# Flamingo block on one core: the order within a slot changed on VectorE, ScalarE and GpSimd, and another interleaving at the end

## The chip, the cores and the metric

The kernel runs on one core of a Trainium2 chip. The metric is the device time of one execution in microseconds (us). TensorE (PE) multiplies matrices, VectorE (DVE) and ScalarE (ACT) do elementwise work and reductions, GpSimd (POOL) a few small operations and some transfers, SyncE (SP) only issues transfers (DMAs).

## The reference

32 sequences x of 128 tokens by 128 channels, each with a context of 77 rows by 96. Cross-attention with 16 heads of 8 channels on the twice normalised x, added back through tanh of a gain; then a mixture of 8 experts of which each token uses 2, added back likewise:

```python
x = x + jnp.tanh(g_xattn[0]) * xattn(_layernorm(x), ctx_768, norm_g, norm_b, tnorm_g, tnorm_b, Wq, bq, Wk, bk, Wv, bv)
#   q = (layer_norm(x) @ Wq + bq), k, v = layer_norm(xf) @ Wk + bk, @ Wv + bv; H = 16, hd = 8
#   w = softmax(q k / sqrt(hd)); y = w v
x = x + jnp.tanh(g_ffn[0]) * ffn(_layernorm(x), w_router, w1, w2)
#   logits = xf @ w_router; top_vals, top_idx = top_k(logits, 2); probs = softmax(top_vals)
#   h = square(relu(xf w1[e])); y_e = h w2[e]; out = sum over the chosen two of y_e * probs
```

## The kernel before

The 32 sequences are cut into S = 8 groups of G = 4 (called s); one sequence of a group is a batch, j = 0 to 3. The program is a software pipeline written out by hand, with one instruction stream for each engine. `steps` runs a step for i = -2 to S + 1, and a step has four slots j. In slot j of step i, `slots` (line 253) names the batches in work: near[k] is the batch k slots away from batch j of group i. For near[2] the maxima of the scores are taken, near[0] gets its transposed scores (scoresT) and exponents, near[-1] the products with v (values), the turn of its heads and the post work on VectorE, near[-2] its transpose (turn), its logits (route) and the low part of x. Beside this, two experts of an older group are computed per slot (`ffn_units`, line 247): hidden (TensorE), gated (u, VectorE), square (hs, ScalarE), output (TensorE); e[1] and e[2] are the two experts, and held is the last expert of the slot before, whose output comes at the start of this slot. From i = 8 on only closing work is left. For the last group the experts are weighed afterwards by `weighed` and have no gates before.

TensorE's tiles for scores, transposes and projections share two banks in turn (`ab_sequence`, line 45): each use waits until the use two before it has been taken (`claim`), unless it is marked free because another wait implies that. Names that follow: negm (line 1003) is the maximum over one part of the scores, s1a to s1d are four parts of a batch, of which a and b come at the end of one slot, c and d at the start of the next. `attended` (line 1017) is the post work in steps: rden, o, x1 (written x<-x_res,o), st, mv. `rstd` on GpSimd makes rs from mv, `normalise2` makes xn from both, `turn` (line 559) transposes xn, `routed` (line 1060) takes top and logits. `gate` (line 1069) makes the gates of a group in slot 1. TensorE turns them (line 574), ScalarE copies them, SP stores them in DRAM and broadcasts them back as gb in three parts, and `gated` (line 1116) reads gb in slot 2. `low_keys` and `low_queries` make k_lo and q_lo in slot 3. `load_rows` (line 1300) is GpSimd's transfer x_res, read by x1 a step later; `load` fetches x and context for three groups ahead in slot 1, behind rstd.

VectorE's stages are Python generators: `take(stage, n)` issues the next n pieces of a stage, so the order of VectorE is the order of the take lines in its `step` (line 1194). Nothing is scheduled automatically.

## Time and profile before

| | |
|---|---|
| time, median of 3 runs (lowest, highest) | 349.1 us (348.03, 349.65) |
| the profiled execution | 348.87 us, of which the span shown is 347.1 |
| TensorE busy | 292.9 us, 84% of the span |
| VectorE, ScalarE, GpSimd busy | 66%, 52%, 31% |
| mean granted TensorE clock | 0.966 of full speed, full speed in each whole step after the start |

A busy time says little about which engine to blame here, since all engines work at once. Read how much TensorE idles in one step, then which instruction of another engine ended each idle time, and then what stood ahead of that instruction on its own engine. In a timeline row the bracket is the idle time ahead of the instruction and what ended it; durations of neighbours can overlap a little, since an engine starts the next instruction while the last one drains.

### The profile page before, as it was taken

The numbers are of one execution on the slowest core, as the hardware profiler recorded it, in microseconds if no ns is written. First come the engines' busy times: TensorE is split into PE (matmuls) and PEld (weight loads), VectorE is DVE, ScalarE is ACT, GpSimd is POOL, SyncE is SP. The second block draws the span as 40 slices with busy tenths as digits, with TensorE's granted clock in tenths as the row PEclk, the third lists the DMA queues.
The fourth block names the chain that finished last, engine by engine and source line by source line (L and its number), as shares of the span: only waits on it lengthen the run. The fifth ranks groups of instructions, "written<-read, shape, count | busy, mean of one in ns | idle before, by whom it ended". The sixth has DMA issues, their size and how long they took to land.

```text
span 347.1 us, 7792 instructions
## 1 busy us (share of the span) xinstructions
PE 292.9 (84%) x2809; PEld 237.6 (68%) x2809; DVE 230.6 (66%) x929; ACT 181.0 (52%) x412; POOL 109.2 (31%) x198
## 2 busy tenths in 40 slices
PE   0867979888889998999899989999999999787695
PEld 0435658666767877777777777777777788675484
DVE  7565275677757775778677757886657656554555
ACT  1331354656455566555655566466556555553373
POOL 6495305147303531343134313421322100211000
PEclk9995587999999999999999999999999999999999
DMA  3243011027343836283629281835273530350011
GB/s 82 79 128 111 19 42 34 17 54 129 118 178 57 126 111 213 53 132 105 216 49 124 54 281 35 117 66 157 115 113 54 153 126 3 81 198 0 0 34 30
DMA packets 18918, 32.92 MB, mean 95 GB/s; under 512 B 4921, under 2 KB 12058, under 8 KB 18880
## 3 DMA queue, kind: packets, MB, share of 16 engines
q1 hardware_dynamic: 12176, 23.39, 28.0%
q0 software_dynamic: 3216, 7.66, 9.2%
q10 hardware_dynamic: 3488, 1.38, 1.5%
q8 instruction: 22, 0.36, 0.5%
q14 instruction: 16, 0.13, 0.2%
HBM read 21.04 MB, written 2.21 MB: 67 GB/s over the span
## 4 chain that ended last, share of the span: by engine, by line
PE 46%; DVE 27%; issue 9%; DMA 6%; ACT 6%; POOL 3%; SPq 2%; DVEq 0%; ACTq 0%; POOLq 0%
PE y L592 10%; PE c L547 8%; DVE u L1122 6%; PE ab L503 4%; DMA gb<-gates_scratch 3%; PE ab L570 2%; DMA qs<-q_lo 2%; PE ab L445 2%; DVE negm L1003 2%; POOL rs L1288 2%; PE s L524 2%; PE ab L453 2%; PE ab L562 2%; PE h L478 2%; PE h L458 2%
## 5 line engine op out<-in xcount | busy, mean ns | idle before, releaser
L1003 DVE TENSOR_REDUCE negm<-ab 128x4 f32<-128x308 f32 x128 | 60.6, 474 | 53.3 <-PE ab L503 52.8
L804 ACT ACTIVATE p<-s 77x512 f32<-77x512 f32 x128 | 74.2, 583 | 17.2 <-PE s L524 17.0
L592 PE MATMUL y<-w2s,hs 128*128 128x128 f32 x448 | 61.0, 280 | 8.2 <-ACT hs L809 8.2
L524 PEld LDWEIGHTS s<-qs,ks 104*77 104x77 f32 x512 | 55.7, 153 | 13.1 <-issue 5.7
L592 PEld LDWEIGHTS y<-w2s,hs 128*128 128x128 f32 x448 | 55.3, 193 | 11.0 <-ACT hs L809 10.3
L524 PE MATMUL s<-qs,ks 104*77 104x128 f32 x512 | 59.7, 241 | 2.0 <-ACT p L804 1.8
L503 PE MATMUL ab<-ks,qs 96*128 96x312 f32 x128 | 51.4, 403 | 4.9 <-DMA qs<-q_lo 1.3
L1286 POOL TENSOR_SCALAR rs<-mv 128x1 f32<-128x1 f32 x32 | 7.4, 230 | 131.3 <-DVE mv L1044 131.2
L809 ACT ACTIVATE hs<-u 128x512 f32<-128x512 f32 x56 | 34.6, 624 | 18.0 <-DVE u L1122 17.8
L1122 DVE SCALAR_TENSOR_TENSOR u<-h,gb 128x512 f32<-128x512 f32 x56 | 36.9, 674 | 1.5 <-DMA gb<-gates_scratch 1.5
L547 PE MATMUL c<-p,vs 77*32 77x128 f32 x1024 | 34.6, 276 | 1.8 <-DVE qs L992 1.8
L585 PE MATMUL h<-x_hi,w_lo 128*128 128x512 f32 x64 | 32.9, 515 | 0.0
L790 ACT ACTIVATE oT<-c 128x256 f32<-128x256 f32 x32 | 12.3, 383 | 38.9 <-PE c L547 38.9
L503 PEld LDWEIGHTS ab<-ks,qs 96*128 96x128 f32 x128 | 25.7, 201 | 8.8 <-issue 2.4
L547 PEld LDWEIGHTS c<-p,vs 77*32 77x32 f32 x1024 | 26.0, 109 | 6.7 <-issue 6.5
L1317 POOL DMA_DIRECT2D ks<-k_lo x32 | 18.3, 577 | 23.0 <-issue 13.7
L586 PE MATMUL h<-x_lo,w_hi 128*128 128x512 f32 x64 | 25.2, 394 | 0.0
L587 PE MATMUL h<-x_hi,w_hi 128*128 128x512 f32 x64 | 25.2, 393 | 0.0
L734 ACT ACTIVATE mT<-ab 32x128 fp32r<-32x128 f32 x32 | 8.4, 262 | 26.2 <-PE ab L509 26.2
L1288 POOL TENSOR_TENSOR rs<-rs,neg_half 128x1 f32<-128x1 f32 x32 | 18.3, 572 | 2.7
L562 PE MATMUL ab<-ident,xn 128*128 128x128 f32 x32 | 9.8, 307 | 9.9 <-DVE xn L1050 9.9
L1279 POOL TENSOR_TENSOR nrm<-nrm,neg_half 77x4 f32<-77x4 f32 (+1 forms) x16 | 17.1, 1067 | 1.3
(127 smaller groups left out, 498.3 us busy)
## 6 DMA issues: line engine op xcount, KB each, us to landing
gb<-gates_scratch SPq DMA_DIRECT2D x14, 768.0 KB, 6.2
gb<-gates_scratch SPq DMA_DIRECT2D x7, 512.0 KB, 4.3
qs<-q_hi SPq DMA_DIRECT2D x12, 256.0 KB, 5.7
ks<-k_hi SPq DMA_DIRECT2D x60, 39.0 KB
x_res<-in_x_dram POOLq DMA_DIRECT2D x8, 256.0 KB, 7.4
out_dram<-y_out POOLq DMA_DIRECT2D x7, 256.0 KB, 6.4
x_sb<-in_x_dram POOLq DMA_DIRECT2D x6, 256.0 KB, 4.8
qs<-q_lo SPq DMA_DIRECT2D x6, 256.0 KB, 7.3
```

The lines of the kernel that those rows point to most:

```text
L503: nc.tensor.matmul(p[:, 0:J * NP].rearrange("t (i n) -> t i n", n=NP), qs[0:QR, par, c, T * j:T * j + T], ks[0:QR, par, c, :, NP * j:NP * ...
L524: mm = nc.tensor.matmul(p[0:N, T * i:T * i + T], ks[:, par, c, i, NP * j:NP * j + N], qs[:, par, c, T * j:T * j + T], start=True, stop=True)
L547: mm = nc.tensor.matmul(bank_c[VT * i:VT * i + VT, r:r + T], vs[:, par, j, NC * i + c, :], p32[:, m % LR, T * i:T * i + T], start=(c == 0) ...
L585: nc.tensor.matmul(p[:, :], w1_lo[:, e, :], x_hi[:, par, :], start=True, stop=False)
L586: nc.tensor.matmul(p[:, :], w1_hi[:, e, :], x_lo[:, par, :], start=False, stop=False)
L587: nc.tensor.matmul(p[:, :], w1_hi[:, e, :], x_hi[:, par, :], start=False, stop=True).then_inc(h_ready, 1)
L592: mm = nc.tensor.matmul(bank_y[:, D * b:D * b + D], hs[:, e % 2, T * b:T * b + T], w2s[:, e, :], start=(e == 0 and b == 0), stop=(e == E - ...
L804: nc.scalar.activation(p32[:, m % LR, :], src, ACT.Exp).then_inc(p_done, 1)
L809: nc.scalar.activation(hs[:, e % 2, :], u[:, e % 2, :], ACT.Square).then_inc(hs_done, 1)
L1003: nc.vector.tensor_reduce(negm[:, :, c], bank_ab[bank][:, 0:J * NP].rearrange("t (i n) -> t i n", n=NP)[:, :, 0:N], AX.X, ALU.max, negate= ...
L1122: nc.vector.scalar_tensor_tensor(out=u[:, e % 2, :], in0=bank_h[e % 2][:, :], scalar=0.0, in1=gb[:, par, e, :], op0=ALU.max, op1=ALU.mult) ...
L1288: nc.gpsimd.tensor_tensor(rs2[:, 1:2], rs2[:, 0:1], neg_half[:, 0:1], ALU.pow).then_inc(post_p, 1)
```

## The change

No instruction is added or taken away; instructions change places within a slot, and at the end between slots. On VectorE the order becomes one of its own for each slot j. ScalarE takes the exponent of part 2 ahead of the copies of v in slot 1, and has an order of its own for i >= S, where it squares first. GpSimd issues x_res behind rstd and the two norms. TensorE keeps its order up to i = 6 but for one more claim: turn 2 now waits for its bank. From slot 2 of i = 7 on, values come ahead of the turn; the output of the first expert of slot 2 moves into slot 3, the gates' transpose of slot 1 behind an output, and in the closing the order of turn, route and outputs changes.

```diff
 # TensorE
-                p, ready = claim(s, f"turn{j}", j != 1 and not last(s))
+                p, ready = claim(s, f"turn{j}", j in (0, 3) and not last(s))
 ... closing
                 if near[-1]:
-                    turn(*near[-2])
                     for c in range(NC):
                         values(*near[-1], c)
+                    turn(*near[-2])
...
                 if near[-1]:
+                    turn_heads(*near[-1])
                     route(*near[-2])
-                    turn_heads(*near[-1])
                 if e[2] is not None:
                     hidden(sf, pf, e[2])
+                if e[1] is not None:
+                    (output_alone if last(sf) else output)(sf, pf, e[1])
                 if near[-2] and not near[-1]:
                     route(*near[-2])
-                if e[1] is not None:
-                    (output_alone if last(sf) else output)(sf, pf, e[1])
 ... step
+                    values_first = i == S - 1 and j > 1
+                    if values_first:
+                        for c in range(NC):
+                            values(*near[-1], c)
                     if near[-2]:
                         turn(*near[-2])
+                    if i == S - 1 and j == 3:
+                        output(held[0], held[1], held[2] - 1)
...
-                    if j == 1 and spread(i - 1):
+                    if j == 1 and spread(i - 1) and i < S - 1:
                         gates_turn(i - 1)
                     if e[1] is not None and j != 2:
-                        output_of(sf, pf, e[1])
+                        output(sf, pf, e[1])
+                    if j == 1 and spread(i - 1) and i == S - 1:
+                        gates_turn(i - 1)
...
-                    if e[1] is not None and j == 2:
-                        output_of(sf, pf, e[1])
+                    if e[1] is not None and j == 2 and i < S - 1:
+                        output(sf, pf, e[1])
 # ScalarE
+                    if i >= S:
+                        if near[-1]:
+                            evacuate_heads(*near[-1])
+                        for one in e[1:]:
+                            if one is not None:
+                                squared(sf, one)
+                            if one == 6 and near[-2]:
+                                evacuate_turned(*near[-2])
+                        if j == 1 and near[-2]:
+                            gate_exp(i - 1)
+                        continue
...
+                    if near[0] and j == 1:
+                        exponent(*near[0], 2)
                     if j == 1 and nxt:
                         evacuate_v(*nxt)
 # VectorE, closing (i >= S)
+                if e[1] is not None and not last(sf):
+                    gated(sf, pf, e[1])
+                take(post, 4)
+                if near[-1]:
+                    routed(*near[-2])
+                    take(post)
+                elif near[-2]:
+                    low_x(*near[-2])
+                if e[2] is not None and not last(sf):
+                    gated(sf, pf, e[2])
+                if near[-1]:
+                    normalise2(*near[-1])
+                    low_x(*near[-2])
+                elif near[-2]:
+                    routed(*near[-2])
+                    take(gating, 7)
 # VectorE, step, behind the maxima of c and d (in slot 3 routed now stands ahead of the one of d)
+                    if j == 1:
+                        take(gating, 3)
+                        if e[1] is not None:
+                            gated(sf, pf, e[1])
+                        take(gating)
+                        take(post)
+                        take(gating)
+                        take(post)
+                        take(gating)
+                        take(post)
+                        take(gating)
+                        ...
+                    if j == 3:
+                        take(post, 2)
                         take(prepare)
                         take(post)
+                        if e[1] is not None and i < S - 1:
+                            gated(sf, pf, e[1])
+                        if near[-1] and i < S - 1:
+                            normalise2(*near[-1])
+                        take(prepare)
+                        if e[2] is not None:
+                            gated(sf, pf, e[2])
 # GpSimd
-                    if j == (2 if i == -1 else 0) and nxt:
-                        load_rows(*nxt)
                     if near[-1]:
                         rstd(*near[-1])
                     if j == (1 if i == 0 else 0) and i != -1 and third:
                         norm_rstd(third[0], "ctx")
                         norm_rstd(third[0], "x")
+                    if j == (2 if i == -1 else 0) and nxt:
+                        load_rows(*nxt)
```

VectorE in slot 1 of a steady step, before; eq and gates are the gate work, x, st and mv the post work of a batch:

```order
L1092 TENSOR_TENSOR eq<-iota,idx_f 128x32 x2
L1098 TENSOR_TENSOR eq<-eq,gt 128x32
L1104 TENSOR_TENSOR eq<-eq 128x32
L1111 TENSOR_TENSOR gates<-eq,gt 128x4x8
L1035 TENSOR_TENSOR x<-x_res,o 128x128
L1040 BN_STATS st<-x 128x6
L1044 BN_AGGR mv<-st 128x2
L1122 SCALAR_TENSOR_TENSOR u<-h,gb 128x512
```

and now:

```order
L1106 TENSOR_TENSOR eq<-iota,idx_f 128x32 x2
L1049 TENSOR_TENSOR x<-x_res,o 128x128
L1112 TENSOR_TENSOR eq<-eq,gt 128x32
L1054 BN_STATS st<-x 128x6
L1118 TENSOR_TENSOR eq<-eq 128x32
L1058 BN_AGGR mv<-st 128x2
L1125 TENSOR_TENSOR gates<-eq,gt 128x4x8
L1136 SCALAR_TENSOR_TENSOR u<-h,gb 128x512
```

The post work (x, st, mv) is threaded between the gate operations, and gates is written after mv.

VectorE in slot 2 of a steady step, before (the last rows of the slot):

```order
L1148 TENSOR_TENSOR y_out<-x,y 128x512
L1044 BN_AGGR mv<-st 128x2
L1122 SCALAR_TENSOR_TENSOR u<-h,gb 128x512 x2
L1003 TENSOR_REDUCE negm<-ab 128x4
L1050 TENSOR_SCALAR xn<-x,mv,rs 128x128
```

and now:

```order
L1162 TENSOR_TENSOR y_out<-x,y 128x512
L1058 BN_AGGR mv<-st 128x2
L1136 SCALAR_TENSOR_TENSOR u<-h,gb 128x512
L1017 TENSOR_REDUCE negm<-ab 128x4
L1136 SCALAR_TENSOR_TENSOR u<-h,gb 128x512
L1064 TENSOR_SCALAR xn<-x,mv,rs 128x128
```

One of the two u now stands behind the first negm.

VectorE at the end, from the last mv to the start of the last group's gates, before:

```order
L1044 BN_AGGR mv<-st 128x2
L1050 TENSOR_SCALAR xn<-x,mv,rs 128x128
L1122 SCALAR_TENSOR_TENSOR u<-h,gb 128x512 x2
L1066 MAX top<-ab 128x8
L1067 COPY logits<-ab 128x8
L1057 TENSOR_TENSOR x_lo<-xT,x_hi 128x128
L1076 TENSOR_TENSOR gt<-top 128x4
L1078 MAX_INDEX index<-top,logits 128x8 x4
```

and now:

```order
L1058 BN_AGGR mv<-st 128x2
L1136 SCALAR_TENSOR_TENSOR u<-h,gb 128x512
L1064 TENSOR_SCALAR xn<-x,mv,rs 128x128
L1071 TENSOR_TENSOR x_lo<-xT,x_hi 128x128
L1136 SCALAR_TENSOR_TENSOR u<-h,gb 128x512
L1071 TENSOR_TENSOR x_lo<-xT,x_hi 128x128
L1136 SCALAR_TENSOR_TENSOR u<-h,gb 128x512
L1080 MAX top<-ab 128x8
L1081 COPY logits<-ab 128x8
L1090 TENSOR_TENSOR gt<-top 128x4
```

Each u now stands as early as it can, and top and logits of the last batch behind the last u.

## Rows read from the trace of the kernel before

**Rows 1.** Busy time by engine in one step (from:to, length, engines).

```profile
204.00:239.60 35.60, 32.41 (x341) 27.26 (x341) 26.65 (x113) 20.84 (x50) 10.26 (x19) 1.00 0.50 106
```

**Rows 2.** Timeline, slot 2 of i = 5: start, duration, instruction, idle ahead.

```profile
238.02 1.25 DVE L1122 SCALAR_TENSOR_TENSOR u<-h,gb 128x512 f32<-128x512 f32 x2
239.19 0.47 DVE L1003 TENSOR_REDUCE negm<-ab 128x4 f32<-128x308 f32 x1
239.80 0.63 PE L436 MATMUL ab<-ident,xn 128*128 128x128 f32 x4 [0.86 <-DVE negm L1003]
```

**Rows 3.** Timeline, slot 3 of i = 4 and the turn that opens i = 5.

```profile
209.25 0.76 PE L445 MATMUL ab<-cnT,wk 96*128 96x308 f32 x2 [0.29 <-DVE logits L1067]
...
213.13 0.75 DVE L982 SCALAR_TENSOR_TENSOR q_lo<-ab,vec,q_hi 128x512 fp32r<-128x512 f32 x1 [1.34 <-ACT q_hi L760]
...
214.40 0.47 DVE L1003 TENSOR_REDUCE negm<-ab 128x4 f32<-128x308 f32 x1
214.78 0.34 DVE L1050 TENSOR_SCALAR xn<-x,mv,rs 128x128 f32<-128x128 f32 x1
...
215.17 0.33 PE L562 MATMUL ab<-ident,xn 128*128 128x128 f32 x1 [0.28 <-DVE xn L1050]
```

**Rows 4.** Timeline, slot 0 of i = 5, GpSimd's transfer, and slot 1's turn.

```profile
221.02 0.79 POOL L1304 DMA_DIRECT2D x_res<-in_x_dram  x1 [4.59 <-DVE st L1040]
...
221.89 0.47 DVE L1003 TENSOR_REDUCE negm<-ab 128x4 f32<-128x308 f32 x1
...
223.17 0.33 PE L562 MATMUL ab<-ident,xn 128*128 128x128 f32 x1 [0.78 <-DVE xn L1050]
```

**Rows 5.** Timeline, slot 1 of i = 5, VectorE, and slot 2's turn.

```profile
229.86 0.21 DVE L1111 TENSOR_TENSOR gates<-eq,gt 128x32 f32<-128x32 f32 x1
230.00 0.29 DVE L1035 TENSOR_TENSOR x<-x_res,o 128x128 f32<-128x128 f32 x1
230.32 0.29 DVE L1040 BATCH_NORM_STATS2 st<-x 128x6 f32<-128x128 f32 x1
230.76 0.18 DVE L1044 BATCH_NORM_AGGREGATE mv<-st 128x2 f32<-128x6 f32 x1
...
232.46 0.33 PE L562 MATMUL ab<-ident,xn 128*128 128x128 f32 x1 [0.56 <-DVE xn L1050]
```

**Rows 6.** Chain at i = 4; landings at i = 3; waits for gb; all landings.

```profile
194.87 2.31 DMA gates_scratch<-gatesT
...
197.19 5.16 DMA gb<-gates_scratch
...
gates_scratch<-gatesT SPq DMA_DIRECT2D x1, 16.0 KB, 1.4
...
gb<-gates_scratch SPq DMA_DIRECT2D x1, 512.0 KB, 4.3
...
DVE u L1122 <- DMA gb<-gates_scratch: 1.5, 2, 0.9
...
DMA to landing us min/median/max: 3.5/5.0/8.2
```

**Rows 7.** Waits from 295 to 331 us: who, total, times, longest.

```profile
PE y L592 <- ACT hs L809: 6.8, 6, 1.6
...
PE ab L562 <- DVE xn L1050: 1.1, 1, 1.1
...
PE h L574 <- DVE gates L1111: 0.9, 1, 0.9
```

**Rows 8.** The end: broadcast of gb, its landing, the first u, an output.

```profile
299.97 1.28 SPq L356 DMA_DIRECT2D gb<-gates_scratch  x3
...
gb<-gates_scratch SPq DMA_DIRECT2D x1, 512.0 KB, 4.6
...
305.38 1.25 DVE L1122 SCALAR_TENSOR_TENSOR u<-h,gb 128x512 f32<-128x512 f32 x2
...
327.09 1.16 PE L592 MATMUL y<-w2s,hs 128*128 128x128 f32 x8 [1.63 <-ACT hs L809]
```

More of the change, by code:

```diff
@@ L640, in step @@
                     sf, pf, held, e = ffn
-                    output_of = output_alone if last(sf) else output
                     if i >= S:
@@ L1192, in _, with closing @@
             dve.wait_ge(const_made, CONSTS)
+            def closing(j, near, ffn, gating, post):
+                sf, pf, held, e = ffn
+                if held and last(held[0]):
+                    weighed(*held)
+                if e[1] is not None and not last(sf):
[14 more added lines that the diff above has]
+                    take(gating, 7)
             def step(i, par):
@@ L1219, in step @@
                         take(prepare, 9)
+                    if i >= S:
+                        closing(j, near, ffn, gating, post)
+                        if j == 2 and not last(i - 2):
+                            finish(i - 2, par)
+                        if e[1] is not None and last(sf):
+                            weighed(sf, pf, e[1])
+                        continue
                     take(top_scores)
@@ L1244, in step @@
                     if j == 2:
+                        take(post, 2)
+                        if exists(i - 2) and i < S - 1:
+                            finish(i - 2, par)
                         take(post)
+                        if e[1] is not None:
+                            gated(sf, pf, e[1])
+                        if i == S - 1:
+                            normalise2(*near[-1])
+                        take(prepare, 2)
+                        if near[3] and i > 0:
+                            take(tops_of(near[3]))
@@ L1246, in step @@
+                        if e[2] is not None:
+                            gated(sf, pf, e[2])
+                        take(prepare)
                     if j == 3:
+                        take(post, 2)
                         take(prepare)
                         take(post)
-                    if e[1] is not None and not (i >= S and near[-2] and not near[-1]):
-                        gated_or_weighed(sf, pf, e[1])
-                    take(gating, 4)
-                    take(post, 3)
-                    take(prepare)
@@ L1254, in step @@
-                    if i >= S and near[-1]:
-                        normalise2(*near[-1])
-                    if e[2] is not None and not last(sf):
-                        gated(sf, pf, e[2])
-                    take(prepare)
-                    if near[3]:
+                        if e[1] is not None and i < S - 1:
+                            gated(sf, pf, e[1])
+                        if near[-1] and i < S - 1:
+                            normalise2(*near[-1])
+                        take(prepare)
@@ L1260, in step @@
+                        if e[2] is not None:
+                            gated(sf, pf, e[2])
+                        take(prepare)
+                    if near[3] and (j != 2 or i <= 0):
                         take(tops_of(near[3]))
-                    if near[-1] and i < S:
+                    if near[-1] and (j < 2 or (j == 2 and i < S - 1) or (j == 3 and i == S - 1)):
                         normalise2(*near[-1])
```

41 lines of the change are left out of this document (20 added, 21 removed).

## The prediction

> **What bounds the kernel now.** Read first the busy time of a full step, then TensorE's waits in it, then the instructions on both sides of each wait. In a step of the steady part TensorE is busy 32.41 of 35.60 us; DVE 26.65, ScalarE 20.84, GpSimd 10.26 [rows 1]. So TensorE sets the pace, a step can lose at most 3.2 us of idleness, and a reorder of the other engines pays only where TensorE waits for them. I number steps by i as the code does; the rows are of i = 4 and 5, and steps 2 to 5 repeat them.
>
> The waits are few. In slot 2 the transposes of the next x wait 0.86 us for a score bank, which the first maximum of the slot (negm) frees; that negm stands behind two gate products u of 1.25 us [rows 2]. In slot 3 the key projection waits 0.29 us for the logits copy, and the turn (transpose of xn) that opens slot 0 waits 0.28 [rows 3]. The turn that opens slot 1 waits 0.78 us: GpSimd spends 0.79 us issuing x_res before the root rs from which xn is made [rows 4]. The turn that opens slot 2 waits 0.56 us, at the end of a DVE run without a gap [rows 5]. Together 2.8 of the 3.2 us. From 295 us on the waits are larger: 6.8 us in six waits for hs, 1.1 for xn, 0.9 for the gates [rows 7].
>
> **The change part by part.** No instruction is added or removed; all terms are waits.
>
> (a) Slot 2: one u now stands ahead of the first negm, the other behind. negm starts one u earlier, half of 1.25, about 0.6 us. The wait of 0.86 shrinks to 0.26 [rows 2]. The second u is 0.4 later, but its square is wanted only after four output matmul pairs and a turn; xn follows it and the turn is 0.6 us earlier too, just when xn is done (u to 239.7, xn 0.35). There are five such slots, i = 1 to 5: 5 x 0.6 = 3.0 us.
>
> (b) Slot 3 into 0: routed (top and logits) now precedes the fourth negm, in time that DVE idles, so the 0.29 wait goes; the key and query chain behind it moves with it. xn stands ahead of q_lo, inside the 1.34 us that DVE waited there for ScalarE. The turn gets a new wait, for the first negm of the slot; queued behind it on TensorE are the outputs of the next expert, so all of slot 0. That negm ended at 214.87 [rows 3]; by the 0.25 us that q_lo comes earlier it ends at 214.6, and the turn starts about 214.7 instead of 215.17. I take 0.45 us; below, the bound is 0.29 (the new wait eats the rest), above 0.57. For i = 1 to 5: 5 x 0.45 = 2.3 us.
>
> (c) Slot 0 into 1: GpSimd does the root and the two norms before it issues x_res. rs can start right after mv, 0.8 us earlier; then the negm ahead of xn is last, ending at about 222.35. The turn moves from 223.17 to 222.7, 0.45 us [rows 4]. x_res is read only a step later, so its delay of 3.5 us (issue behind two roots) costs nothing. For i = 2 to 6: 5 x 0.45 = 2.3 us; slot 0 of i = 1 waits for a transfer of q and is not counted.
>
> (d) Slot 1 into 2: x1, st and mv are threaded between the small gate operations. st to mv takes 0.44 us with nothing between though st lasts 0.29, while gates to x1, which are independent, takes 0.14 [rows 5]. With the dependent pairs filled, the u behind starts 0.4 us sooner and mv 0.55 sooner. The turn at 232.46 gains 0.45; its wait of 0.56 bounds it. The gates are finished 0.45 us later, which TensorE meets as a wait of up to 0.3 before the gates' transpose, inside the 0.56. ScalarE's exponent ahead of the copies of v frees its part sooner. For i = 2 to 6: 5 x 0.45 = 2.25 us, between 0 and 2.8.
> The Trainium skill ("VectorE: DVE Perf Modes", section "The DRAIN you can't avoid") speaks against this: the pipeline flush is paid after every DVE operation, a semaphore after each costs nothing extra, so there would be nothing to fill. By it (d) would keep only xn's 0.2 us wait for rs, 5 x 0.2 = 1.0 us; the rows above disagree with it, 0.44 against 0.14, and I go by them.
>
> (e) What stands against (a) to (d): the gates go through DRAM and come back broadcast (gb), and the first u of slot 2 needs them. In i = 4 the store took 2.31 and the broadcast 5.16 us and u waited; u waited for gb twice, 1.5 us in all, at most 0.9 (i = 1), so 0.6 in i = 4. In i = 3 the same two took 1.4 and 4.3 [rows 6], which leaves a slack of 7.47 - 0.6 - 5.7 = 1.2 us. The change stores the gates 0.1 us later and wants u 0.45 earlier. And GpSimd's loads for i + 3, which follow rs, start 0.55 us sooner, on top of the store instead of behind it, in i = 1 to 4. i = 4 gives back 0.55. For i = 2 and 3 I take an even chance that they go as i = 4 did (7.47 - 5.7 = 1.8, less 1.2 slack, plus 0.55: 1.2 each), so 1.2 in all; with 0.1 for i = 1, 1.9 us. Bounds: 0.6, and with the slowest gb seen, 8.2 us, far more (below).
>
> (f) In slot 3 of i = 6 there is no q_lo to cover xn's wait for rs: loss 0.15 us.
>
> (g) The end. At i = 7 the values of the batch go ahead of the turn and the first expert's output moves behind it. The waits for gates (0.9) and xn (1.1) are then mostly filled: route comes about 1.5 us sooner. But gb for this step is limited: it was issued at 299.97, landed after 4.6 us, and u started at 305.38, so 0.8 us of slack [rows 8]; the gates' transpose is 0.5 us later now, behind an output. gb lands at 305.1, u starts there, the square, the outputs of two experts and route follow with nothing idle between: 1.5 us gained up to there, of the 3.0 in three waits. The other five waits for hs (1.0, 1.4, 1.0, 1.6, 0.6, which is 6.8 less the first of 1.1) have one cause: u stood behind top, logits and the post work, and the last but one square stood on ScalarE behind the turn's copies and the gates' exponents; the 327.09 output waited 1.63 us so [rows 8]. Now u comes first, squares first, and the gate work last. What is late next is TensorE itself: the hidden products of 0.9 us and outputs of 0.9 us each cover u and hs (0.68 + 0.63 plus hops). I take 5.3 of 5.7, for a hop here and there. Gates end when DVE next needs them, with the first weighing, a little ahead of its output. Sum for the end 6.8 us; bounds 3 (half of the squares still wait, for a chain of xn, turn, x_lo) and 8.4.
>
> Sum: 3.0 + 2.3 + 2.3 + 2.25 - 1.9 - 0.15 + 6.8 = 14.6 us. The profiled execution took 348.87 us (span 347.1 and 1.8 around it), 0.2 below the median of 349.1. 348.87 - 14.6 = 334.3, on the median's footing 334.5 us.
>
> **The rivals.**
> 1. The gates' round trip sets slot 2. For: two steps already wait, and slack elsewhere is 1.2 us or less; against: i = 5 and later have no loads beside it. If store and gb take 2.5 + 5.2 = 7.7 us in i = 1 to 4 (6.5, 5.7, 5.7 and 7.5 before): 1.2, 1.4, 1.4 and 0.8 lost, 4.9 instead of 1.9: 337.5 us.
> The Trainium skill ("DMA: Bandwidth & Descriptors", sections "Latency and other measured facts" and "Issuing engines are not separate DMA queues") says a small transfer's time is mostly the receipt from HBM, longer under load, and that transfers of all issuers share the engines. The spread of 1.4 to 2.3 us for the same 16 KB store fits it; it is this rival's mechanism.
> 2. The end yields half (3 us instead of 6.8): squares wait on the chain xn, turn, x_lo that moved behind u. For: POOL's root still takes its time between mv and xn; against: u and hs no longer depend on it. 338.3 us.
> 3. Filling the dependent gaps on DVE gains nothing, (d) is 1.0: 335.7 us. Against: the spacings in rows 5.
> 4. The gains are given back: TensorE's waits reappear at the new bank waits and transfers, as in (b); 348 to 350 us. Against: each shrunken wait has its next cause above.
> 5. Slower. Loads, store and broadcast pile up so that gb takes its slowest, 8.2 us [rows 6], after a store of 2.5: 10.7 us in all, and u, all of DVE behind it and the bank TensorE wants wait. Lost: 4.2, 4.5, 4.5, 3.8 in i = 1 to 4 and 3.6 at i = 7, 20.6 us against gains of 16.5 gross: 353 us. It decides from 16.5 / 5 = 3.3 us lost in each of the five. Against: 8.2 belongs to a 768 KB part, this one has 512.
>
> **How the numbers follow.** Forecast 334.5 us, 331 to 337 if its mechanisms hold: 0.60. Rival 1: 0.13. Rival 2: 0.09. Rival 3: 0.05. Rival 4: 0.04. Rival 5: 0.03. Better than 331 (the end at its bound of 8.4, gb unhindered): 0.06. A measurement of this kernel tells about 0.5% (1.7 us) from no change. Faster by more: 0.60 + 0.13 + 0.09 + 0.05 + 0.06 = 0.93; same 0.04; slower 0.03. Range for 8 in 10: 330 to 341, where the low end takes in the upper bound of the end and the high end rivals 1 and 2, alone or together.
>
> **What the profile after would show.** (a) TensorE's x transposes wait about 0.3 us in slot 2; 0.8 again would say that gb or the second u holds negm. (b) No wait for logits. (c) GpSimd's rs within 0.3 us of mv, turn waits near 0.3. (d) mv before gates, under 0.3 us at the slot 2 turn, perhaps a wait at the gates' transpose. (e) Count u's waits for gb: two of 0.6 to 1.2 us fit, four or more over 1 us are rival 1. (g) After about 305 us the waits for hs fall from six with 6.8 us to under 1.5 us in all. Steps of 33.7 us and an end shorter by 6 to 7 us confirm the sum; steps still of 35 us refute it.

## The result and the profile after

The changed kernel takes 333.9 us in the median (328.17 to 337.06, four runs) beside 348.9 us (348.03 to 349.65, four runs) of the kernel before: a ratio of 0.948, 95% interval 0.935 to 0.960. The ratio counts only executions within 1.5% of the fastest of their kernel, here 328.17 and 332.87 us of the changed one, so it lies below the 0.957 of the two medians. The forecast was 334.5 us. The executions of the changed kernel lie 9 us apart; those before lie 1.6 us apart here, but over all later sets they span 344.3 to 354.1 us. So single executions of either kernel are not to be compared by their total; why they spread is told below. The profiled execution is the fastest of the four, 328.17 us with a span of 326.4, so it shows 20.7 us of difference where the medians show 15.0.

The first thing to take out is the start. These rows are the first turn (transpose of xn) of the program, before and then after:

```profile
57.74 0.27 PE L562 MATMUL ab<-ident,xn 128*128 128x128 f32 x1
```

```profile
53.88 0.33 PE L562 MATMUL ab<-ident,xn 128*128 128x128 f32 x1
```

Up to there both programs are the same, and yet 3.86 us lie between them. The busy times of two stretches say why (from:to, length, engines in the order PE, PEld, DVE, ACT, POOL, then the granted TensorE clock), before and after:

```profile
30.00:36.00 6.00, 5.12 (x20) 4.06 (x20) 3.17 (x12) 1.03 (x3) 1.61 (x3) 0.50 0.41 117
36.00:42.00 6.00, 5.48 (x18) 3.87 (x18) 1.85 (x5) 2.72 (x6) 1.25 (x3) 0.50 0.02 7
```

```profile
30.00:36.00 6.00, 4.93 (x20) 3.73 (x20) 3.20 (x13) 1.42 (x3) 1.62 (x3) 0.59 0.41 117
36.00:42.00 6.00, 5.72 (x25) 3.30 (x25) 2.58 (x6) 4.47 (x9) 2.64 (x5) 1.00 0.10 33
```

In both the clock fell to the lower level, 1.2 GHz, after TensorE idled around 24 us; it came back at about 35 us in one execution and 43 us in the other. That is no part of the change. The kernel before seems to have such starts too: two of its later executions, with a mean clock of 0.975 and 0.974 instead of 0.966, took 344.27 and 344.81 us, 4 to 5 us less than the profiled one.

From the first turn on the difference is 16.8 us. I read it from the starts of the 32 turns (L562), as time saved in us between one turn and the next:

| turn to turn | i = 1 | 2 | 3 | 4 | 5 | 6 |
|---|---|---|---|---|---|---|
| slot 0 to 1 | 0.42 | 0.36 | 0.39 | 0.38 | 0.38 | 0.49 |
| slot 1 to 2 | 0.18 | 0.81 | 0.83 | 0.84 | 0.84 | 0.83 |
| slot 2 to 3 | 0.86 | -0.58 | 0.60 | 0.80 | 0.60 | 0.01 |
| slot 3 to the next 0 | 0.47 | 0.46 | 0.46 | 0.46 | 0.23 | -0.13 |

With -0.19 in i = 0, -0.18 from slot 0 to 1 of i = 7 and 6.22 from there to the end that makes 16.8. One step, to be laid beside [rows 1]:

```profile
203.70:237.30 33.60, 32.12 (x341) 27.29 (x341) 26.68 (x112) 20.90 (x50) 10.74 (x20) 1.00 0.53 120
```

The step is 2.0 us shorter with the same 341 matmuls in it; TensorE idles 1.5 us of it instead of 3.2. The four places, in the order of the prediction. Slot 2 of i = 5, which answers to [rows 2]: negm behind one u, and the transposes wait 0.27 us instead of 0.86.

```profile
225.38 0.66 DVE L1136 SCALAR_TENSOR_TENSOR u<-h,gb 128x512 f32<-128x512 f32 x1
...
225.96 0.47 DVE L1017 TENSOR_REDUCE negm<-ab 128x4 f32<-128x308 f32 x1
226.34 0.68 DVE L1136 SCALAR_TENSOR_TENSOR u<-h,gb 128x512 f32<-128x512 f32 x1
226.57 0.63 PE L436 MATMUL ab<-ident,xn 128*128 128x128 f32 x4 [0.27 <-DVE negm L1017]
```

Slot 3 of i = 4 into slot 0 [rows 3]: neither the key projection nor the turn has a bracket any more, but the query projection now waits 0.41 us for mT where it waited 0.18 for k_lo, a wait that the prediction did not name. In i = 5 it waits 0.7 us for k_lo, and there slot 3 gave 0.23 us instead of 0.46.

```profile
197.84 0.69 PE L445 MATMUL ab<-cnT,wk 96*128 96x308 f32 x2
...
200.03 1.10 PE L453 MATMUL ab<-xnT,wq 128*128 128x512 f32 x2 [0.41 <-ACT mT L737]
...
203.76 0.30 PE L562 MATMUL ab<-ident,xn 128*128 128x128 f32 x1
```

Slot 0 of i = 5 into slot 1 [rows 4]: rs starts 0.21 us after mv ends (209.59 + 0.18), x_res has left for 213.66, and the turn waits 0.31 us instead of 0.78.

```profile
209.59 0.18 DVE L1058 BATCH_NORM_AGGREGATE mv<-st 128x2 f32<-128x6 f32 x1
...
209.98 0.22 POOL L1359 TENSOR_SCALAR rs<-mv 128x1 f32<-128x1 f32 x1 [4.79 <-DVE mv L1058]
...
211.38 0.33 PE L562 MATMUL ab<-ident,xn 128*128 128x128 f32 x1 [0.31 <-DVE xn L1064]
...
213.66 0.87 POOL L1377 DMA_DIRECT2D x_res<-in_x_dram  x1
```

Slot 1 of i = 5 into slot 2 [rows 5]: from the first eq to the u behind the gate work it is now 217.16 to 218.32, 1.16 us, where it was 228.94 to 230.86, 1.92 us, for the same instructions. The turn has no wait left.

```profile
217.16 0.28 DVE L1106 TENSOR_TENSOR eq<-iota,idx_f 128x32 f32<-128x32 f32 x2
217.36 0.28 DVE L1049 TENSOR_TENSOR x<-x_res,o 128x128 f32<-128x128 f32 x1
217.56 0.18 DVE L1112 TENSOR_TENSOR eq<-eq,gt 128x32 f32<-128x32 f32 x1
217.68 0.29 DVE L1054 BATCH_NORM_STATS2 st<-x 128x6 f32<-128x128 f32 x1
217.89 0.17 DVE L1118 TENSOR_TENSOR eq<-eq 128x32 f32<-128x32 f32 x1
218.12 0.18 DVE L1058 BATCH_NORM_AGGREGATE mv<-st 128x2 f32<-128x6 f32 x1
218.22 0.21 DVE L1125 TENSOR_TENSOR gates<-eq,gt 128x32 f32<-128x32 f32 x1
218.32 0.69 DVE L1136 SCALAR_TENSOR_TENSOR u<-h,gb 128x512 f32<-128x512 f32 x1
...
219.83 0.33 PE L562 MATMUL ab<-ident,xn 128*128 128x128 f32 x1
```

The store of the gates leaves 7.72 us behind the turn of slot 1 (211.38), where it left 8.04 us behind it (223.17). Before and after:

```profile
231.21 0.33 SPq L349 DMA_DIRECT2D gates_scratch<-gatesT  x1
```

```profile
219.10 0.33 SPq L349 DMA_DIRECT2D gates_scratch<-gatesT  x1
```

The end [rows 7, 8]. Of the waits for hs, 6.8 us in six, 1.3 us in three are left from 275 to 311 us, the wait for gates is gone, and of the 1.1 us for xn 0.2 is left. But the last group's broadcast is late: its store left 8.17 us behind the turn of slot 1, where it left 7.55 before. u waits for it, and so TensorE's values wait 1.95 us for the exponent p: from i = 7 on the change puts the square hs of slot 2 ahead of p on ScalarE, an edit that the text on the change does not list.

```profile
290.34 0.69 DVE L1136 SCALAR_TENSOR_TENSOR u<-h,gb 128x512 f32<-128x512 f32 x1 [1.39 <-DMA gb<-gates_scratch]
291.06 0.63 ACT L812 ACTIVATE hs<-u 128x512 f32<-128x512 f32 x1 [2.24 <-DVE u L1136]
...
291.60 0.57 ACT L807 ACTIVATE p<-s 77x512 f32<-77x512 f32 x1
...
292.23 0.43 PE L547 MATMUL c<-p,vs 77*32 77x128 f32 x8 [1.95 <-ACT p L807]
```

The waits for gb are four now (i = 1, 2, 4, 7: 0.64, 1.06, 0.41, 1.39 us), 3.5 us in all, where two made 1.5 [rows 6].

### The profile page after: what moved, and what is told of

Its sections match the earlier page's. It is cut to its first block, busy times and chain, and to the rows that moved or that the text cites. A ratio compares the mean times of both kernels' runs of the same rounds, so it can differ in the third digit from the quotient of the medians.

```text
span 326.4 us, 7799 instructions
## 1 busy us (share of the span) xinstructions
PE 286.0 (88%) x2809; PEld 235.2 (72%) x2809; DVE 234.1 (72%) x929; ACT 180.8 (55%) x412; POOL 109.4 (34%) x198
## 4 chain that ended last, share of the span: by engine, by line
PE 53%; DVE 24%; DMA 8%; issue 7%; ACT 5%; POOL 1%; ACTq 0%; DVEq 0%; POOLq 0%
PE y L592 13%; PE c L547 8%; DMA gb<-gates_scratch 6%; PE ab L503 5%; DVE u L1136 4%; PE s L524 3%; DVE negm L1017 3%; PE ab L570 2%; DVE m_parts L1024 2%; DMA gates_scratch<-gatesT 2%; PE ab L562 2%; PE h L458 2%; PE ab L453 2%; PE h L478 2%; PE ab L436 2%
## 5 line engine op out<-in xcount | busy, mean ns | idle before, releaser
L524 PEld LDWEIGHTS s<-qs,ks 104*77 104x77 f32 x512 | 55.0, 150 | 9.8 <-issue 2.3
L524 PE MATMUL s<-qs,ks 104*77 104x128 f32 x512 | 58.3, 237 | 0.6 <-ACT p L807 0.6
L1136 DVE SCALAR_TENSOR_TENSOR u<-h,gb 128x512 f32<-128x512 f32 x56 | 38.0, 678 | 5.0 <-DMA gb<-gates_scratch 3.5
L547 PE MATMUL c<-p,vs 77*32 77x128 f32 x1024 | 35.7, 280 | 3.7 <-ACT p L807 1.9
L1390 POOL DMA_DIRECT2D ks<-k_lo x32 | 18.3, 578 | 21.6 <-issue 12.4
L1361 POOL TENSOR_TENSOR rs<-rs,neg_half 128x1 f32<-128x1 f32 x32 | 18.3, 572 | 2.7
L1064 DVE TENSOR_SCALAR xn<-x,mv,rs 128x128 f32<-128x128 f32 x32 | 12.3, 383 | 7.0 <-POOL rs L1361 6.7
## 6 DMA issues: line engine op xcount, KB each, us to landing
qs<-q_hi SPq DMA_DIRECT2D x12, 256.0 KB, 5.9
x_res<-in_x_dram POOLq DMA_DIRECT2D x8, 256.0 KB, 4.0
out_dram<-y_out POOLq DMA_DIRECT2D x7, 256.0 KB, 6.3
x_sb<-in_x_dram POOLq DMA_DIRECT2D x6, 256.0 KB, 4.4
qs<-q_lo SPq DMA_DIRECT2D x6, 256.0 KB, 7.4
```

The source lines that it names most:

```text
L524: mm = nc.tensor.matmul(p[0:N, T * i:T * i + T], ks[:, par, c, i, NP * j:NP * j + N], qs[:, par, c, T * j:T * j + T], start=True, stop=True)
L547: mm = nc.tensor.matmul(bank_c[VT * i:VT * i + VT, r:r + T], vs[:, par, j, NC * i + c, :], p32[:, m % LR, T * i:T * i + T], start=(c == 0) ...
L1136: nc.vector.scalar_tensor_tensor(out=u[:, e % 2, :], in0=bank_h[e % 2][:, :], scalar=0.0, in1=gb[:, par, e, :], op0=ALU.max, op1=ALU.mult) ...
L1361: nc.gpsimd.tensor_tensor(rs2[:, 1:2], rs2[:, 0:1], neg_half[:, 0:1], ALU.pow).then_inc(post_p, 1)
```

## The experiments

"Four steps" is the time from the turn of slot 0 of i = 2 to that of i = 6: 143.14 us before (107.65 to 250.79), 135.28 after (102.05 to 237.33). "The end" runs from the turn of slot 1 of i = 7 to the end of the span: 56.09 before, 49.87 after. Some of the expectations place four steps at slot 1 instead, which moves the numbers by 0.1 us at most. A ratio is always to the kernel before in the same set. Since executions of one kernel lie up to 10 us apart, the totals do not size the single edits; their sizes are read from the slots of one profiled execution each.

**The changed kernel again.** 

> The changed kernel, unaltered, again. Theory: its executions differ in how long TensorE is at its lower clock in the first 60 us (granted clock 0.972 with a span of 326.4 us, 0.954 with 335.3), not in the steps after. Each us more at the low clock costs 0.7 us. Then spans of 326 to 336 us again, in the order of their clocks, and in the profile four steps (turn of i = 2 to turn of i = 6) of 135.3 us again, 7.9 less than before, and 49.9 us from the turn of i = 7, slot 1, to the end, 6.2 less than before. Rival: the spread comes from waits for gb in the steps; then the four steps differ by some us between profiles.

Measured: 334.4 us (331.06 to 338.0), ratio 0.964, interval 0.946 to 0.983. Four steps 135.38 as expected, so in these two profiles the steps do not make the difference. But the end took 51.74 instead of 49.9, 1.87 longer than in the first profile, so the first 60 us are not all of it either. The clock shows where:

```profile
288.00:294.00 6.00, 3.80 (x54) 2.91 (x53) 3.32 (x12) 2.82 (x5) 1.59 (x3) 1.00 0.94 304
294.00:300.00 6.00, 6.00 (x38) 5.65 (x39) 1.69 (x7) 2.49 (x7) 0.00 (x0) 0.72 0.23 91
```

```profile
293.51 0.43 PE L547 MATMUL c<-p,vs 77*32 77x128 f32 x8 [2.20 <-ACT p L807]
```

TensorE was busy 3.80 of 6 us with the wait of 2.20 us at its end, and right after it the clock was at the lower level for some 3.4 us (0.72 over 6 us). Here the wait for the broadcast cost twice.

**Part (a) undone: both u of slot 2 in a row.**

```diff
                             normalise2(*near[-1])
+                        if e[2] is not None and i < S - 1:
+                            gated(sf, pf, e[2])
                         take(prepare, 2)
...
-                        if e[2] is not None:
+                        if e[2] is not None and i == S - 1:
                             gated(sf, pf, e[2])
```

> Slot 2 with both u ahead of the first maximum again (a undone), all else as changed. Theory: TensorE's wait at the x transposes is 0.86 us again where gb is in time, 0.6 more in each of i = 1 to 5, so the four steps take 137.6 us instead of 135.3, and the whole 3 us more. Rival: an earlier second u gives back what the maximum loses (its square and output come sooner), under 1 us in all.

Measured: 338.1 us (335.56 to 340.28), ratio 0.977, interval 0.963 to 0.991. In i = 5 slot 2 lasts 8.71 us as before (8.70), against 8.10, with the old wait back:

```profile
231.97 1.25 DVE L1136 SCALAR_TENSOR_TENSOR u<-h,gb 128x512 f32<-128x512 f32 x2
...
233.76 0.63 PE L436 MATMUL ab<-ident,xn 128*128 128x128 f32 x4 [0.86 <-DVE negm L1017]
```

So (a) is 0.6 us a slot, as worked out. Four steps took 139.30, 4.0 more, not 2.3: in i = 2 the late gb and the two u add up to a wait of 2.17 us, after which the clock falls (0.72 over 129 to 135 us). In i = 1, ahead of the four steps, the same happened behind 1.68 us (0.60 and 0.83 in 93 to 99 us). So with one u ahead of negm a late gb makes a shorter wait: 1.44 us in i = 2 of the changed kernel.

**Part (d) undone on VectorE: gate work and post work each in a row.**

```diff
-                        take(gating)
-                        take(post)
-                        take(gating)
-                        take(post)
-                        take(gating)
-                        take(post)
-                        take(gating)
+                        take(gating, 4)
+                        take(post, 3)
```

> Slot 1 with the gate work and then the post work in one piece each, as before, all else as changed (d undone on VectorE). Theory, filled gaps between dependent operations: the turn that opens slot 2 comes 0.45 us later or more, a wait of about 0.5 us for xn stands ahead of it, and the four steps take 1.8 to 2.5 us more; gb is waited for less, since the gates are ready 0.45 us sooner. Rival, the rule that the flush after each operation cannot be filled: st to mv would be no dearer than any other pair, the four steps grow by 0.8 us at most (xn's wait for rs).

Measured: 335.2 us (334.04 to 336.36), ratio 0.967, interval 0.955 to 0.978. Slot 1 to 2 lasts 9.31 us in the mean of i = 2 to 5, against 8.45 changed and 9.28 before, and the turn waits 1.03 us:

```profile
220.70 0.28 DVE L1106 TENSOR_TENSOR eq<-iota,idx_f 128x32 f32<-128x32 f32 x2
221.10 0.19 DVE L1112 TENSOR_TENSOR eq<-eq,gt 128x32 f32<-128x32 f32 x1
221.33 0.19 DVE L1118 TENSOR_TENSOR eq<-eq 128x32 f32<-128x32 f32 x1
221.63 0.21 DVE L1125 TENSOR_TENSOR gates<-eq,gt 128x32 f32<-128x32 f32 x1
...
222.63 0.66 DVE L1136 SCALAR_TENSOR_TENSOR u<-h,gb 128x512 f32<-128x512 f32 x1
...
224.25 0.33 PE L562 MATMUL ab<-ident,xn 128*128 128x128 f32 x1 [1.03 <-DVE xn L1064]
```

The same instructions take 1.93 us when each waits for the one ahead and 1.16 us when they alternate. Undone, this edit takes back 0.86 us, all that slot 1 had gained; a flush paid after every operation alike, with nothing to fill, is refuted for these operations. Only 1.8 us of the 3.4 show in four steps (137.04), since slot 2 is 0.42 shorter in turn: the step comes later to a gb that is then in time. The total shows nothing of this edit, 335.2 beside 334.4 us of the changed kernel in the same set.

**Part (d) undone on ScalarE: the exponent of slot 1 behind the copies of v.**

```diff
-                    if near[0] and j == 1:
-                        exponent(*near[0], 2)
                     if j == 1 and nxt:
                         evacuate_v(*nxt)
...
-                    if near[0] and j != 1:
+                    if near[0]:
                         exponent(*near[0], 2)
```

> ScalarE's exponent of part 2 in slot 1 behind the copies of v and of mT again, all else as changed. Theory: the 0.83 us gained per slot 1 (0.45 forecast) has its other 0.38 from here; TensorE waits 0.24 us again for p ahead of scoresT and the square of the first expert is later, so the four steps take 1.0 to 1.6 us more. Rival: the turn waits for xn from VectorE anyway, and the exponent's place is worth under 0.2 us per step; then all 0.83 came from VectorE.

Measured: 337.7 us (331.73 to 340.36), for which no ratio is given. Slot 1 is 8.58 us in the mean against 8.45: in slot 1 this edit is worth 0.13 us, and the rival holds there. It also moves the gates' store, which leaves 8.03 or 8.04 us behind the turn of slot 1 again in i = 2 to 6, as in the kernel before, instead of 7.72. In i = 5 that turn starts at 220.47 and the store here:

```profile
228.50 0.33 SPq L349 DMA_DIRECT2D gates_scratch<-gatesT  x1
```

So the exponent's place is what lets the store leave 0.32 us sooner. The rest of the difference are waits for gb (6.4 us in five) and two falls of the clock behind waits of 2.13 and 2.24 us; the later store has a share in these waits from i = 2 on, but not in the 2.10 us of i = 1, where it left as early as in the changed kernel. How much of the total is the edit's stays open.

**Part (c) undone: x_res ahead of rs.**

```diff
+                    if j == (2 if i == -1 else 0) and nxt:
+                        load_rows(*nxt)
                     if near[-1]:
                         rstd(*near[-1])
...
-                    if j == (2 if i == -1 else 0) and nxt:
-                        load_rows(*nxt)
```

> Undoes one edit: GpSimd puts x_res back ahead of rs in slot 0. Theory (the prediction's part c): rs comes later by the load's issue, TensorE waits for u at slot 1's opening again by about 0.4 us in each step, four steps from slot 1 of i=2 last 136.8 to 137.0 us instead of 135.3 to 135.4, and the time is about 2.5 us above the changed kernel (336 to 337 us beside 334). Rival: rs was no longer what came last in slot 0 and the load's place is worth nothing; then four steps stay at 135.3 and slot 1's opening shows no new wait.

Measured: 336.0 us (334.31 to 338.63), ratio 0.970, interval 0.960 to 0.980. Slot 0 to 1 is 8.13 us against 7.62, and the chain is the old one:

```profile
215.10 0.79 POOL L1377 DMA_DIRECT2D x_res<-in_x_dram  x1 [4.56 <-DVE st L1054]
215.91 0.24 POOL L1359 TENSOR_SCALAR rs<-mv 128x1 f32<-128x1 f32 x1
...
217.24 0.33 PE L562 MATMUL ab<-ident,xn 128*128 128x128 f32 x1 [0.80 <-DVE xn L1064]
```

It was 0.51 a step where I expected 0.4, and it is xn, not u, that TensorE waits for; I had named the wrong waiter. Undone it costs more than (c) gained, 8.13 against 7.99 us in the kernel before. Four steps took 140.18 because of a gb wait of 2.61 us in i = 2, where the first part of the broadcast took 7.0 us, and the half clock behind TensorE's wait of 2.98 us.

**The end alone: before's order up to i = 6.** The steps i < 7 issue VectorE's old order (its old `step`, kept beside the new one), GpSimd's x_res and ScalarE's exponent stand where they stood; TensorE keeps the new bank wait of turn 2.

```diff
+                if i < S - 1:
+                    step_old(i, par)
+                    return
...
-                    if near[0] and j == 1:
+                    if near[0] and j == 1 and i >= S - 1:
```

> The order of before on every engine up to i=6, the changed order from i=7 on alone. Theory (the prediction's part g stands by itself): four steps from slot 1 of i=2 last 143.1 us as before, and from slot 1 of i=7 to the end 49.9 us instead of 56.1, so about 343 us, ratio 0.982. Rival: the end's gain needs the steps' gain (x and u of the last step come early only in the changed order), then the end gives 3 us or less and the time is 346 us or more.

Measured: 343.5 us (341.03 to 346.88, ten runs), ratio 0.988, interval 0.983 to 0.993. The end is 49.85 us, 6.2 less than before, and the slots 0, 1 are at 7.99 and 9.29 as before. The end's gain stands by itself and adds to that of the steps. Four steps took 145.25: the old pair of u meets a gb that is later still in i = 4 (u waits 1.03 us for it instead of 0.62), TensorE waits 2.03 us where it waited 1.60 in the profile before, and the clock falls behind it (0.59 over 206 to 209 us):

```profile
204.67 0.73 PE L436 MATMUL ab<-ident,xn 128*128 128x128 f32 x4 [2.03 <-DVE negm L1017]
```

**The loads for i + 3 later.** They are issued when the broadcast is under way, in slot 2, behind a wait for the reciprocal of that slot.

```diff
+                    if j == 2 and i > -1 and exists(i + 3):
+                        pool.wait_ge(post_d, at(POST, G * near[-1][0] + near[-1][2], "recip"))
+                        load(i + 3, 1 - par)
                     if near[-1]:
                         rstd(*near[-1])
...
-                    if j == (3 if i == -1 else 1) and i > -2 and exists(i + 3):
+                    if i == -1 and j == 3 and exists(i + 3):
                         load(i + 3, 1 - par)
```

> GpSimd issues the loads for i+3 in slot 2, when the gates have been broadcast, instead of in slot 1 ahead of them. Theory: these loads (1.6 MB in a burst) are what makes the gates' store and broadcast slow in four of the steps; without them the store lands in 1.4 us and the broadcast in 4.3 or less in every step, VectorE waits for the broadcast under 1 us in all in i=1 to 5, the stretches at half clock that follow these waits are gone, and the time is 331 to 333 us beside 334. Rival: the store is slow by itself, whatever is loaded beside it; then the waits for gb stay at 4 to 5 us in all, and the later loads make nothing better or hold up rows of i+3.

Measured: 329.9 us (328.06 to 330.92), ratio 0.953, interval 0.946 to 0.960; four steps 133.75. The issues around slot 1 of i = 4, changed kernel and then this one (size, us to landing):

```profile
gb<-gates_scratch SPq DMA_DIRECT2D x1, 512.0 KB, 5.1
gates_scratch<-gatesT SPq DMA_DIRECT2D x1, 16.0 KB, 1.7
```

```profile
gb<-gates_scratch SPq DMA_DIRECT2D x1, 512.0 KB, 3.5
gates_scratch<-gatesT SPq DMA_DIRECT2D x1, 16.0 KB, 2.2
```

Half of the theory holds. The broadcast's first part lands in 3.5 to 3.7 us in i = 1 to 4, where it took 4.1 to 5.6; the waits for gb in i = 2 and 4 are gone (0.61 us stays in i = 1), and four steps give 1.5 us. At i = 7, where no loads are, the wait is as in the changed kernel, 1.33 us, the clock is at 0.50 in 291 to 294 us, and the end takes 51.33 us. The store is not faster (2.4, 1.7, 1.4, 2.2 us in i = 1 to 4 against 1.9, 1.8, 1.4, 1.7): what makes it slow in these steps stays open, and the loads are not it. (The loads are 371.5 KB a step, x 256.0 and context 115.5, not the 1.6 MB that I wrote.)

**The gates' transpose of i = 7 ahead of the output again.**

```diff
-                    if j == 1 and spread(i - 1) and i < S - 1:
+                    if j == 1 and spread(i - 1):
                         gates_turn(i - 1)
...
-                    if j == 1 and spread(i - 1) and i == S - 1:
-                        gates_turn(i - 1)
```

> At i=7 alone the transpose of the gates goes back ahead of the output of slot 1, as in all other steps. Theory: at the end it is the broadcast that comes last for slot 2 of i=7; with the transpose some 0.6 us earlier, gb is issued 0.5 to 1 us earlier, VectorE waits 0.4 to 0.9 us for it instead of 1.4 to 1.6, TensorE waits for p under 1.5 us instead of 2.0 to 2.2, and the end from slot 1 of i=7 takes 49.0 to 49.5 us instead of 49.9. Rival: TensorE stands for the gates at the transpose for as long as was won, the end is the same within 0.2 us.

Measured: 331.1 us (328.58 to 331.97), ratio 0.956, interval 0.950 to 0.963; the end 49.39 us.

```profile
284.52 0.28 PE L574 MATMUL h<-ident,gates 128*32 128x128 f32 x1 [1.18 <-DVE gates L1123]
...
290.72 0.69 DVE L1134 SCALAR_TENSOR_TENSOR u<-h,gb 128x512 f32<-128x512 f32 x1 [0.44 <-DMA gb<-gates_scratch]
...
292.61 0.42 PE L547 MATMUL c<-p,vs 77*32 77x128 f32 x8 [1.02 <-ACT p L805]
```

TensorE stands 1.18 us for the gates, but then 1.02 instead of 1.95 for p, and the broadcast leaves 0.4 us sooner (9.14 instead of 9.57 us behind the turn of slot 1). So the changed kernel's late transpose cost 0.5 us here, beside the half clock that can follow 2 us of waiting.

**The later loads and the transpose ahead again, and p ahead of hs in slot 2 of i = 7.** The diff shows the third edit alone.

```diff
-                    if e[1] is not None and (j != 2 or i >= S - 1):
+                    if e[1] is not None and j != 2:
                         squared(sf, e[1])
...
-                    if e[1] is not None and j == 2 and i < S - 1:
+                    if e[1] is not None and j == 2:
                         squared(sf, e[1])
```

> Three edits on the changed kernel: the loads for i+3 in slot 2 behind the gates' broadcast, the gates' transpose of i=7 ahead of the output, and in slot 2 of i=7 ScalarE's exponent p ahead of hs, as in the steps before. Theory: the last wait for p at i=7 is made of VectorE's wait for gb and of hs standing ahead of p; with all three TensorE waits under 0.6 us there (1.0 with the transpose alone, 1.9 with the loads alone), the end from slot 1 of i=7 takes 48.5 to 49.0 us, four steps 133.7, no stretch at half clock after 60 us, and the time is 328 us (327 to 330). Rival: the broadcast of i=7 is slow by itself and exponent p ahead of hs only moves the wait to hs and the output; the end stays at 49.4 and the time is that of the loads alone, 330.

Measured: 330.5 us (329.1 to 331.72), ratio 0.954, interval 0.947 to 0.960, beside a before of 347.3 in the same set. Four steps 133.74 and the end 48.53 us, both as expected; one wait for gb is left, 0.5 us. Yet the time is above the 328 expected and not below that of the later loads alone: this execution got its full clock back only after 42 us and lost it twice more, in 72 to 78 and in 84 to 90 us (0.72 each), with no TensorE wait above 1.3 us from 60 us up to there. The lengths of steps and end were predicted, the clock of the first 90 us was not.

**The same with seven matmuls more at the start.**

```diff
+                    if i == -1 and j in (2, 3):
+                        keep_on(bank_s2[1], 5 if j == 2 else 2)
                     if near[2]:
                         max_turn(*near[2])
```

> The same kernel with seven more matmuls of the kind that fills TensorE's waits at the start (five in slot 2 and two in slot 3 of i=-1, results unused). Theory: the half clock between 24 and 33 to 42 us follows TensorE's idle time at 20 to 30 us; with the extra matmuls the granted clock stays at 1.00 there or comes back at 30 us in every execution, the first turn of i=1 comes at 67 to 69 us instead of 70 to 73, the executions lie within 2 us of one another, and the time is 325 to 327 us. Rival: the clock falls there whatever is filled in, and the matmuls cost their own time, 0 to 2 us more than without them.

Measured: 323.0 us (322.83 to 324.23), ratio 0.932, interval 0.926 to 0.938, the fastest kernel here, and its executions lie 1.4 us apart. The stretches of the start:

```profile
24.00:30.00 6.00, 4.85 (x21) 3.07 (x19) 4.95 (x13) 0.53 (x2) 5.49 (x9) 1.00 0.39 103
30.00:36.00 6.00, 5.19 (x35) 4.20 (x36) 4.28 (x13) 2.95 (x5) 1.75 (x3) 1.00 0.39 119
36.00:42.00 6.00, 4.99 (x21) 2.39 (x19) 2.61 (x5) 4.45 (x8) 3.28 (x6) 1.00 0.29 77
```

TensorE is busy 4.85 us from 24 to 30 where it was 2.57 without them, and the clock stays at 1.00. It is still at half between 42 and 50 us, and again from 319 us to the end. Four steps 134.17, the end 48.43.

**The seven matmuls on the changed kernel, and on the kernel before.**

> The changed kernel with these seven matmuls alone. Theory: as with the kernel before it in this set, the start gains 1 to 4 us, but the executions still spread by 4 to 6 us, since the half clocks that follow the waits for gb at i=1, 2 and 7 stay; time 330 to 333 us. Rival: the spread of the changed kernel comes from the first 60 us alone; then its executions lie within 2 us of one another here.

> The kernel before with the same seven matmuls at the start and nothing else. It takes the start's chance out of the comparison: with the changed kernel and these matmuls (327.3 us) it shows what the change itself is worth. Theory: the first turn of i=1 comes at 67.3 to 67.6 us instead of 73.65, the steps and the end stay as before (four steps 143.1, end 56.1), so 341 to 343 us, and the change is worth 14 to 16 us from the same start. Rival: part of the changed kernel's gain stood on lucky starts in the profiled run; then this kernel is at 338 us or less and the change is worth 11 us or less.

Measured: 327.3 us (325.11 to 329.06), ratio 0.941, interval 0.935 to 0.948; and 342.2 us (341.02 to 346.4), ratio 0.978, interval 0.971 to 0.986. The first is less than the 330 to 333 us expected, the second as expected. The matmuls take 6.5 us off the changed kernel (333.9, in another set) and 8.3 off the kernel before (350.5 in its set). The first turns of i = 1 start at 67.40 and 66.44 us, instead of 69.98 and 73.65. From nearly the same start the two kernels are 14.9 us apart by their times and 13.0 by their ratios (0.941 to 0.978, of 342), since they ran in different sets and on different chips: the change is worth 13 to 15 us here, and no lucky start made it. The changed kernel's executions span 4 us instead of 10 (328.17 to 338.0 over its eight). What is left of the spread goes with the wait for gb at i = 7, in this profile 1.81 us on VectorE, then 2.37 on TensorE, then the clock (0.64 over 288 to 294 us), with an end of 53.16 us.

## Why the prediction was right, point by point

The time, 334.5 against 333.9 us, is right to 0.6 us, and the sum of 14.6 us stands beside 15.0 between the medians and 13 to 15 from the same start. The measurement is not that sharp: the ratio of 0.948 stands for 18.3 us, that of the repeat, 0.964, for 12.4. The terms are less exact than their sum, and the closeness of the sum is in part luck.

- (a) Held: 0.60 us in i = 3 and 5, and 0.6 lost again when undone. In i = 4 it gave 0.80.
- (b) Held: 2.1 us in five slots, predicted 2.3; it was undone only together with the others, when the end stood alone (slot 3 of i = 2, 3 and 5 at 9.62 or 9.63 us again instead of 9.16 to 9.40), so its share is argued from the waits that went.
- (c) Held: 2.0 us in five, predicted 2.3; undone, 0.51 a step.
- (d) Mis-sized: 4.15 us in five slots, predicted 2.25. The step that failed is "the u behind starts 0.4 us sooner" and "its wait of 0.56 bounds it". I had filled only the gap of the post work, 0.44 against 0.14 [rows 5]. The chain of gate operations has the same gaps, and with both filled u started 0.76 us sooner. The bound failed too: with VectorE's part undone the turn waited 1.03 us, not 0.56, so TensorE had come to it earlier, in part by ScalarE's exponent (0.13), and a gain of 0.83 was there to be had. Rival 3 is refuted. At the gates' transpose the matmuls show no wait up to i = 6; the weight loads ahead of them waited 0.2 us in each of five steps. The gates came 0.15 us later behind the turn of slot 1, not 0.45.
- (e) The mechanism held, the size was mixed. The store was taken to leave 0.1 us later; in i = 2 to 6 it left 0.32 us sooner, by the exponent's new place, and at i = 7 0.62 later. Slot 2 as a whole (a with e) gave 2.3 us where 1.1 was predicted. Only i = 2 lost, 1.2 us below the 0.6 of its neighbours, as priced; i = 3 lost nothing, i = 4 gave a little and i = 1 gained 0.86. At i = 7 I had gb's landing as the limit, and it was: u waited 1.39 us for it. What I did not see is who stands behind u there, ScalarE's p and with it TensorE. Rival 1 has come in part, with four waits, though two of them under 0.65. Against rival 5 I had said that only a 768 KB part took 8.2 us; with x_res ahead of rs again a 512 KB part took 7.0, and u waited 2.61 us. Neither rival 4 nor rival 5 came.
- (f) Held: 0.13 us in slot 3 of i = 6 where 0.15 was predicted. Slot 0 of i = 7 lost another 0.18, which no term has.
- (g) Right in size: 6.2 of 6.8 us, all of it kept when the end stood alone. The waits for hs fell to 1.3 us in three, under the 1.5 that was set as the mark; rival 2 is refuted. The late transpose of the gates and hs ahead of p cost 1.34 us together (49.87 to 48.53), more than the 0.6 us missing. I had allowed for the transpose's 0.5 us, but not for the exponent behind hs.
- What the sum left out: single executions of the changed kernel lose 1.5 to 3 us again when the clock falls behind a wait for gb. Of the nine profiles with TensorE's and ScalarE's order of the changed kernel at i = 7 it fell there in five, behind waits of 1.51 to 2.37 us. Steps and end of the profiled run alone give 16.8 us, while 15.0 show between medians. So I had the gain in (d) and in slot 2 too small, and a cost that I had not priced made up for it; that it is the clock is shown in single profiles, not for every run. The forecast owes part of its precision to that.

## What to carry to other kernels

Where short dependent operations of one engine stand in a row and other independent ones stand behind them, alternate them: here the same eight instructions took 1.16 us instead of 1.93. Fill the gaps of both chains, not only of the one that the next engine waits for. Before one transfer is wanted earlier, look at what another engine puts beside it: moving 371.5 KB of loads behind the broadcast gave 1.5 us in four steps. When executions of one program lie apart by more than a per cent, read the granted clock in each before reading any edit out of their difference, and compare by the distances between fixed points of the program.

## What the runs showed of the hardware

- After a wait of TensorE of 1.5 to 3.0 us in an otherwise full stretch, the granted clock was at 1.2 GHz for 3.4 us, once for 6.8, and where it fell at i = 7 the end was 1.5 to 3.3 us longer: seen after 1.51, 1.68, 1.89, 1.93, 2.03, 2.13, 2.17, 2.20, 2.24, 2.37 and 2.98 us. Not after every one: 1.95 us in the first profile of the changed kernel, 2.04 us in the kernel before with the seven matmuls, and 1.81, 1.99, 2.05, 2.07 and 2.13 us in other runs left it at full speed. It also fell in one kernel with no wait above 1.3 us ahead of it (in 72 to 78 and 84 to 90 us). So the length of the wait alone does not decide; what does is open.
- At the start the time at half clock differs between executions of the same instructions: the clock was back at 35 or 36 us in some, after 41 to 43 us in others. Seven unused matmuls kept it up from 24 to 42 us and took 6.5 and 8.3 us off the two kernels, between medians of different sets for the first.
- A store of 16 KB took 1.4 us in most steps and 1.5 to 2.5 in others, also with the loads moved away from it; 3.2 us in i = 5 of two runs. The first part of the broadcast, 512 KB, took 4.1 to 5.6 us in i = 1 to 4 of the changed kernel, once 7.0 with x_res ahead of rs, and 3.5 to 3.7 with the loads behind it.
